# The two sums of states of a pair of channel blocks: added by an accumulating DMA instead of TensorE

## What is computed

```python
xz = xn @ W_in                       # 256 -> 1024
xb, z = split(xz)                    # 512 channels each
xb = silu(conv3(xb))
dt = softplus(xb @ W_dt + b_dt)
for n in range(16):                  # states
    h_n[t] = exp(dt[t] * A[:, n]) * h_n[t-1] + dt[t] * xb[t] * B[t, n]
y = sum_n h_n * C[:, n]
y = (y + D_param * xb) * silu(z)
x = x + ga * (residual + y @ W_out)
```

## Time and profile before

| Engine | busy us | share of the span |
|---|---|---|
| TensorE, matmuls (weight loads) | 2303.2 (1648.3) | 87% (63%) |
| VectorE | 2385.8 | 91% |
| ScalarE | 1489.0 | 56% |
| GpSimd | 2255.9 | 86% |
| DMA, queue of GpSimd / of SyncE | | 51.2% / 36.9% of 16 engines |

### The profile page before, as it was taken

How to read it: one execution, slowest core, us unless ns; L and a number is a source line. 1 busy time by engine, 2 the same in 40 slices (tenths; PEclk the granted TensorE clock), 3 DMA queues, 4 the chain that set the end, 5 groups by cost and what they waited for, 6 DMA issues and landing times.

```text
span 2635.9 us, 28145 instructions
## 1 busy us (share of the span) xinstructions
PE 2303.2 (87%) x8814; PEld 1648.3 (63%) x8814; DVE 2385.8 (91%) x2390; ACT 1489.0 (56%) x2825; POOL 2255.9 (86%) x1591
## 2 busy tenths in 40 slices
PE   6356998989989898998989899898989999898799
PEld 2224675756667576666757666575666667576678
DVE  4999999999999999999999999999999999999922
ACT  5656556565655656565565656556565665654320
POOL 2888999998999899899989998999889899988812
PEclk9677999999999999999999999999989999899899
DMA  6998999989999998989999898998989899898911
GB/s 167 256 218 209 216 224 215 235 207 243 214 219 222 210 243 200 248 215 219 222 206 248 192 246 211 224 224 207 249 193 235 209 229 233 200 249 192 233 49 48
DMA packets 312886, 558.72 MB, mean 212 GB/s; under 512 B 46864, under 2 KB 157456, under 8 KB 312736
## 3 DMA queue, kind: packets, MB, share of 16 engines
q0 software_dynamic: 77568, 260.08, 51.2%
q1 hardware_dynamic: 235168, 296.84, 36.9%
HBM read 295.10 MB, written 10.06 MB: 116 GB/s over the span
## 4 chain that ended last, share of the span: by engine, by line
PE 46%; POOL 20%; DVE 13%; issue 9%; ACT 7%; DMA 5%; SPq 0%; POOLq 0%; DVEq 0%
PE wbank L509 17%; PE mbank L521 9%; POOL unit L1361 8%; DVE hbank L765 7%; PE wbank L410 6%; DMA gsum<-unit 4%; PE wbank L451 4%; PE wbank L536 3%; POOL gsum L1375 3%; POOL act L1328 2%; ACT z L939 2%; POOL stat L1249 2%; ACT hbank L1133 2%; PE wbank L435 1%; PE wbank L471 1%
## 5 line engine op out<-in xcount | busy, mean ns | idle before, releaser
L1361 POOL TENSOR_TENSOR unit<-dtx,b_bc 128x1024 f32<-128x1024 f32 x512 | 1417.3, 2790 | 36.5 <-DVE dtx L842 27.9
L765 DVE TENSOR_TENSOR_SCAN hbank<-hbank,unit 128x1024 f32<-128x1024 f32 x512 | 1173.3, 2292 | 50.3 <-ACT hbank L1133 46.6
L1133 ACT ACTIVATE hbank<-dt,a_neg 128x512 f32<-128x512 f32 x1024 | 669.1, 681 | 241.9 <-DVE unit L778 240.0
L1375 POOL DMA_DIRECT2D gsum<-unit x480 | 560.2, 1167 | 73.1 <-DMA gsum<-unit 35.8
L778 DVE TENSOR_TENSOR unit<-hbank,c_bc 128x1024 f32<-128x1024 f32 x480 | 585.4, 1220 | 22.5
L521 PE MATMUL mbank<-down_t,act 128*128 128x256 f32 x2048 | 525.0, 394 | 27.0 <-POOL act L1328 25.9
L509 PE MATMUL wbank<-h_t,up_t 128*128 128x256 f32 x2048 | 509.9, 394 | 37.7 <-DVE xb L636 27.2
L1328 POOL TENSOR_TENSOR act<-act,w_all 128x512 f32<-128x512 f32 x256 | 410.0, 1602 | 142.0 <-DVE act L743 128.2
L509 PE MATMUL wbank<-h_t,gate_t 128*128 128x256 f32 x2048 | 487.3, 381 | 6.3 <-DVE xb L636 5.6
L521 PEld LDWEIGHTS mbank<-down_t,act 128*128 128x128 f32 x2048 | 398.7, 198 | 148.6 <-issue 51.5
L509 PEld LDWEIGHTS wbank<-h_t,up_t 128*128 128x128 f32 x2048 | 397.8, 197 | 141.3 <-DVE xb L636 38.8
(11 more groups left out here) (140 smaller groups left out, 2210.8 us busy)
## 6 DMA issues: line engine op xcount, KB each, us to landing
gsum<-unit POOLq DMA_DIRECT2D x480, 512.0 KB, 7.9
b_bc<-bc_scratch SPq DMA_DIRECT2D x352, 256.0 KB, 7.2
c_bc<-bc_scratch SPq DMA_DIRECT2D x352, 256.0 KB, 7.2
w_all<-w_scratch SPq DMA_DIRECT2D x256, 256.0 KB, 4.9
ht<-in_L_attn_x_dram SPq DMA_DIRECT2D x16, 512.0 KB, 6.1
w_out<-in_L_attn_W_out_dram SPq DMA_DIRECT2D x16, 512.0 KB, 8.0
ht<-in_L_attn_x_dram POOLq DMA_DIRECT2D x16, 512.0 KB, 8.0
out_dram<-xt SPq DMA_DIRECT2D x16, 512.0 KB, 3.1
```

Source lines behind the costliest of these rows:

```text
L765: eng.tensor_tensor_scan(h, h, unit[:, g % RING, :, :].rearrange("p a t -> p (a t)"), 0.0, ALU.mult, ALU.add).then_inc(scanned, 1)
L1133: eng.activation(hbank[g % HB][:, a, :], dt[:, 2 * q + a, :], ACT.Exp, scale=a_neg[:, 2 * q + a, n:n + 1]).then_inc(decayed, 1)
L1361: eng.tensor_tensor(unit[:, g % RING, :, :], dtx[:, 2 * q:2 * q + 2, :], b_bc[:, s:s + 1, :].to_broadcast([P, 2, T]), ALU.mult).then_inc(d ...
L1375: eng.dma_start(gsum[:, 2 * pair + k, :, :], unit[:, g % RING, :, :], accum_op=ALU.add).then_inc(summed[pair][k], 16)
```

## The change

TensorE's `mix` is gone, with its four takes from the ring of banks per sequence. A new step on GpSimd, `merge`, waits for both sums of a pair and issues a DMA that adds `gsum[2 * pair + 1]` onto `gsum[2 * pair]`. VectorE's `mix` waits for its landing and multiplies both blocks of the pair at once, 128x1024, with both operands in SBUF. Waits that pointed to a bank of `y` now point to the semaphores `merged` and `gated`, or, for the buffer xb, to its own readers.

```diff
+        merged, gated = [sem(f"merged{pair}") for pair in range(2)], sem("gated")
...
-                plan += [("mix1", behind, 4, 6, 14), ("load_gb", behind, 1, 45, 58),
+                plan += [("merge1", behind, 1, 3, 3), ("mix1", behind, 1, 10, 10), ("load_gb", behind, 1, 45, 58),
...
-                     ("mix0", slot, 4, 84, 91)]
+                     ("merge0", slot, 1, 82, 82), ("mix0", slot, 1, 90, 90)]
...
             def project(row):
-                    y = work.at["y", row, DK - 1]
-                    need.wait_ge(y.free, y.after)
+                    need.wait_ge(gated, 2 * (row + 1))
...
-            def mix(row, pair):          # on TensorE
-                p = 2 * row + pair
-                for a in range(2):
-                    q = 2 * pair + a
-                    t = fill(("y", row, q))
-                    for k in (1, 0):
-                        need.wait_ge(summed[pair][k], 16 * ADDED[k] * (row + 1))
-                        m = eng.matmul(t.bank[:, :], ident[:, :], gsum[:, (2 * p + k) % SUMS, a, :], start=k == 1,
-                                       stop=k == 0)
-                    m.then_inc(t.full, 1)
...
             def mix(row, pair):          # on VectorE
-                for q in (2 * pair, 2 * pair + 1):
-                    t = work.at["y", row, q]
-                    need.wait_ge(t.full, t.after)
-                    eng.tensor_tensor(gz[:, q, :], gz[:, q, :], t.bank[:, :], ALU.mult).then_inc(t.free, 1)
+                t, blocks = work.at["gate", row, 2 * pair + 1], gz[:, 2 * pair:2 * pair + 2, :]
+                need.wait_ge(t.free, t.after)
+                need.wait_ge(merged[pair], 16 * (row + 1))
+                eng.tensor_tensor(blocks, blocks, gsum[:, 2 * pair, :, :], ALU.mult).then_inc(gated, 1)
...
             def base(row, pair):         # on ScalarE
-                        y = work.at["y", row - 1, 2 * pair + 1]
-                        need.wait_ge(y.full, y.after)
+                        need.wait_ge(merged[pair], 16 * row)
...
+            def merge(row, pair):        # on GpSimd
+                for k in range(2):
+                    need.wait_ge(summed[pair][k], 16 * ADDED[k] * (row + 1))
+                eng.dma_start(gsum[:, 2 * pair, :, :], gsum[:, 2 * pair + 1, :, :], accum_op=ALU.add).then_inc(
+                    merged[pair], 16)
```

More of the change, by code:

```diff
@@ L329, in last_streams @@
             last = NB - 1
-            plan = [("mix1", last, 4, 5, 5), ("project", last, 4, 6, 6),
+            plan = [("merge1", last, 1, 3, 3), ("mix1", last, 1, 5, 5), ("project", last, 4, 6, 6),
                     ("stats", last, 5, 6, 9), ("turn", last, 4, 16, 17), ("load_gb", last, 1, 19, 26),
@@ L526, in experts @@
                         yield
-            def mix(row, pair):
-                p = 2 * row + pair
-                for a in range(2):
-                    q = 2 * pair + a
-                    t = fill(("y", row, q))
-                    for k in (1, 0):
-                        need.wait_ge(summed[pair][k], 16 * ADDED[k] * (row + 1))
-                        m = eng.matmul(t.bank[:, :], ident[:, :], gsum[:, (2 * p + k) % SUMS, a, :], start=k == 1,
-                                       stop=k == 0)
-                    m.then_inc(t.full, 1)
-                    yield
-                    yield
             def modulation(c):
@@ L594, in _ @@
                         "step_sizes0": lambda r: step_sizes(r, 0), "step_sizes1": lambda r: step_sizes(r, 1),
-                        "mix0": lambda r: mix(r, 0), "mix1": lambda r: mix(r, 1),
                         "project": project, "turn": turn, "weigh": weigh, "chunks": lambda r: turning}
@@ L633, in silu_inputs @@
                     if row >= 2:
-                        y = work.at["y", row - 2, q]
-                        need.wait_ge(y.full, y.after)
+                        need.wait_ge(dtx_made, 2 * (row - 1))
+                        for made in base_made:
+                            need.wait_ge(made, 2 * (row - 1))
                     eng.scalar_tensor_tensor(out=xb[:, xb_at(row, q), :], in0=t.bank[:, :], scalar=1.0, in1=cv, op0=ALU.add,
@@ L775, in times_c @@
                 if u == 0 and row:
-                    y = work.at["y", row - 1, 2 * pair + 1]
-                    need.wait_ge(y.full, y.after)
+                    need.wait_ge(gated, 2 * row + pair - 1)
                 eng.tensor_tensor(o, hbank[g % HB][:, :, :],
@@ L781, in mix @@
             def mix(row, pair):
-                for q in (2 * pair, 2 * pair + 1):
-                    t = work.at["y", row, q]
-                    need.wait_ge(t.full, t.after)
-                    eng.tensor_tensor(gz[:, q, :], gz[:, q, :], t.bank[:, :], ALU.mult).then_inc(t.free, 1)
-                    yield
-                    yield
+                t, blocks = work.at["gate", row, 2 * pair + 1], gz[:, 2 * pair:2 * pair + 2, :]
+                need.wait_ge(t.free, t.after)
+                need.wait_ge(merged[pair], 16 * (row + 1))
+                eng.tensor_tensor(blocks, blocks, gsum[:, 2 * pair, :, :], ALU.mult).then_inc(gated, 1)
+                yield
             def turn_chunks():
@@ L1331, in experts @@
                     yield
+            def merge(row, pair):
[3 more added lines that the diff above has]
+                    merged[pair], 16)
+                yield
             def scale_wo(row):
@@ L1393, in _ @@
                         "step_sizes1": lambda r: step_sizes(r, 1), "stats": stats, "scale_wo": scale_wo,
+                        "merge0": lambda r: merge(r, 0), "merge1": lambda r: merge(r, 1),
                         "scale_h": scale_h}
```

## The result

The changed kernel takes 2723.39 us in the median (2721.1 to 2726.91, 4 runs) against 2642.73 us (2637.07 to 2643.57, 4 runs) of the kernel before beside it: a ratio of 1.0317, 95% interval 1.0299 to 1.0335. It is 81 us slower; 2661 was predicted, with 2698 as the upper end. The profiled execution has a span of 2723.5 us, 87.6 more than before; the profiled execution of before was one of its quicker ones.

What follows compares the result with a forecast made beforehand. VectorE, 96% busy, was taken as the bound. The terms -2 + 42 - 30 + 5 + 3 gave +18 us, 2655.6 us for the profiled execution and 2661 us on the median; range 2618 to 2698.

Steps and rivals of the forecast that it cites:

- GpSimd and the queue: GpSimd's 32 new issues and the 32 transfers of 512 KB on its queue: +5 us, bounds 0 to +37.
- The gaps before scans 4, 7 and 9 go, -30: VectorE's waits at units 4, 7 and 9 vanish (-25 us), and half the router's wait (-5 us).
- ScalarE's own queue made them: Sign of being wrong: if gaps at scans 7 and 9 stay, ScalarE's own queue is their cause.
- The multiplications stand 1.4 and 1.3 us, +42: VectorE's new products, for pairs 0 and 1, wait out GpSimd's products at SBUF: +42 us, bounds 0 to +73.
- That sentence: Argument against GpSimd becoming the bound: each wait of VectorE gives GpSimd the same time back.
- rival B: GpSimd becomes the bound, at units 2 to 6: about +43 us, 2686 us; chance 0.13.
- VectorE's own work, -2: Four products from PSUM become two of 128x1024 from SBUF: -2 us over 16 sequences, bounds -2 to +3.
- The landing, 0: The new DMA lands before VectorE's product can start: no more cost while landings stay under 9 us.
- one of the prediction's own signs of being wrong: At the new product, VectorE stands waiting for a DMA.
- The end, +3: After the last sum lands, DMA and product delay the final projection: +3 us, to +4.

Runs made afterwards that it cites:

- a1: The changed kernel with pair 0's product one unit later (moment 91 for 90): 2732.63 us, ratio 1.0342.
- a3: a1 without the merging DMA; the product waits for both sums and takes the first alone: 2658.37 us, ratio 1.0070.
- a2: a1 with the product's second operand read from the scan's PSUM bank instead of the sum in SBUF: 2731.7 us, ratio 1.0342.
- a4: a2 without the merging DMA, the sums left out of the result: 2661.81 us, ratio 1.0078.
- b1: The kernel before with TensorE's eight additions per batch element on one column instead of 512: 2640.24 us, ratio 0.9993.
- d2: a4 with GpSimd making dtx of pair 1 behind the expert's product of unit 4 instead of ahead of it: 2651.78 us, ratio 1.0047.
- b2: The kernel before with its additions and products moved to the places of the new products: 2668.05 us, ratio 1.0090.
- c2: The changed kernel with pair 1's merging DMA two moments later and its product three moments later: 2811.77 us, ratio 1.0638.
- c4: a2 with a merging DMA of one element per partition instead of 1024: 2704.65 us, ratio 1.0237.
- d1: The changed kernel with GpSimd making dtx of pair 1 behind the expert's product of unit 4 instead of ahead: 2719.26 us, ratio 1.0296.

## Why the prediction was wrong

The direction was right and the size a fourth of it, outside the range. By its steps:

- *"GpSimd and the queue: 0.3 us per sequence, +5 us; bounds 0 to +37"* is the step that failed. It measures 74 us (a1 less a3) and 70 (a2 less a4). I argued that GpSimd's lateness reaches VectorE only through a unit's product and found 2.4 us of air there. It reaches VectorE by three ways, and which of them takes the time depends on the kernel. One is that product after all: scans wait for it 24.3 us in a1 and 35.8 in a2, 3.6 before. The second is VectorE's gated product, which stands longer beside a later GpSimd (1953 ns in a3, 2918 in a1); in the kernel after, most of the loss stands here. The third was not looked for: GpSimd's expert's product, TensorE's L521 in front of the projection, ScalarE's read in front of the decays. The air on that way is 0.66 us, and it could be read from the trace of before. It carries about half of a2's loss per sequence (scan 7's wait 0.40 to 3.11 us) and 0.46 us per sequence of the kernel after.
- *"The gaps before scans 4, 7 and 9 go, -30"* failed too. It rested on TensorE's own queue allowing an earlier projection. TensorE waits for GpSimd at once when it has less to do: b1, the relief alone, is worth 0. The projection came 6.6 us after scan 4 (mean of 15) instead of the 3.0 worked out, and 5.0 before. The gap before scan 4 (0.28 us in the mean) did go, but the one before scan 7 grew from 0.40 to 0.86 us, the one before scan 9 stayed (1.10 to 1.01). The prediction's reading of such a gap, "ScalarE's own queue made them", fails as well: in d2, with an earlier projection, it is 0.25.
- *"The multiplications stand 1.4 and 1.3 us, +42"*: the mechanism is there and even larger, (3004 - 1224) x 32 = 57 us of VectorE's time, 2.0 us in the mean for pair 0 and 1.6 for pair 1. As a term of the sum it fails, since a kernel without it (a2) is no faster than the one with it (a1). What VectorE loses there GpSimd gets. That sentence stood in the prediction, against rival B, and I did not apply it to the term of 42. That 57 and the 20.7 us for landings come near the measured loss in the kernel after is no proof that they make it.
- *VectorE's own work, -2*: the free product lasts 1.22 us as worked out from L842.
- *The landing, 0*, as long as it stays under 9 us: pair 1's takes 4.8 to 8.9 us and costs nothing but at the end, pair 0's 8.6 to 10.6. VectorE waits 20.7 us, 13.3 of them in 14 sequences for pair 0's and 7.4 at the end. This was one of the prediction's own signs of being wrong.
- *The end, +3*: the last product waits to 2591.87 and the projection starts 15.7 us after the last scan's start, against 14.3; this part is +1.4. The projection then takes 6.73 us instead of 3.69, at a granted clock of 0.55 (the last row). From the last scan's start to the end it is 146.0 us against 141.3, +4.7.

```profile
2591.87 1.22 DVE L769 TENSOR_TENSOR gz<-gz,gsum 128x1024 f32<-128x1024 f32 x1 [7.41 <-DMA gsum<-gsum]
...
2593.19 6.73 PE L451 MATMUL wbank<-w_out,gz 128*128 128x256 f32 x16 [8.07 <-issue]
...
2593.00:2600.00 7.00, 6.81 (x17) 5.48 (x18) 0.09 (x1) 0.00 (x0) 0.00 (x0) 0.55 0.00 0
```

- *Rival B* had the right engine and the right place, units 2 to 6, and a price of 43 where some 80 was due. Its test, waits of scans for GpSimd of tens of us, is not met in the kernel after (4.0 us), whose VectorE stands at its own product, and is met in a1 (24.3) and a2 (35.8).

What stays open: why b1 and b2 together cost twice their sum (the wait for the up-projection's bank is where it shows, not why), what moving one product by a unit would cost in c2 without the port, and by which transfers the 512 KB cost 27 us; sums land in 8.1 us in the median in a2 and in 7.9 in c4, which is little to explain it.

## What to carry to other kernels

When the fullest engine is fed by others that are 90% busy, work can't be priced by the engine that does it alone. Take the point where it waits, follow the wait back through every engine to the first that does not wait, and price the slack on each link: here a link two engines away had 0.66 us of slack, and VectorE's 96% said nothing of it. Expect the wait to move when one way is closed: from the product to the scans in a2, from scan 7 to the router in d1 and d2. Relief of an engine is worth only what it brings forward at its next wait for another; if it waits there already, or soon after, the relief turns into idle time, and on TensorE it can be followed by a lower clock (mean 0.949 before, 0.939 in b1). And two costs that are each other's waiting time (VectorE's hold and GpSimd's lateness) must not be added.
